# A decoder layer on one core: the cross layer's main loop begun four steps earlier, and the whole-row norms' bias formed by ScalarE

## The reference

```python
x = x + attn(_layernorm(x), Wqkv_w, Wqkv_b)         # 16 heads of 32, rotary, causal
x = x + xattn(_layernorm(x), ctx_2048, ...)         # a second norm _ln inside
x = x + ffn(_layernorm(x), w_gate_up, w_proj)       # ternary weights, silu, rms norm

def _L0_xattn_ref(...):
    ln_out = _ln(hidden_states, ln_w, ln_b)
    q  = _ln(_fp8_linear(ln_out, wq, q_in_scale))   # 8 groups x 2 heads x 128; k and v the same
    core = _gqa(q, k, v)                            # self half ("S")
    qx = _ln(_fp8_linear(ln_out, wqx, qx_in_scale))
    kx, vx = split(cond @ w_kv_x.T); kx = _ln(kx)
    xout = _gqa(qx, kx, vx)                         # context half ("X")
    catq = _div_clamp_fp8(cat([core, xout]), proj_smooth)
    return catq @ wproj.T * (proj_in_scale * proj_w_scale)
```

## Time and profile before

| | |
|---|---|
| median of 3 runs | 1286.97 us |
| lowest, highest | 1284.61, 3284.15 us |
| the profiled execution | 1285.17 us, its span 1283.4 |
| mean granted TensorE clock | 0.971 |
| PE busy | 1206.2 us, 94% |
| DVE busy | 943.5 us, 74% |
| ACT busy | 796.1 us, 62% |
| POOL busy | 624.7 us, 49% |

### The profile page before, as it was taken

One profiled execution on the slowest core, in us unless ns is written; L12 is line 12 of the kernel. 1 busy time (PEld: TensorE's weight loads), 2 busy tenths in 40 slices (PEclk: granted clock), 3 DMA queues, 4 the chain that ended last, 5 costly groups with the idle time before them and its releaser, 6 DMA issues.

```text
span 1283.4 us, 19499 instructions
## 1 busy us (share of the span) xinstructions
PE 1206.2 (94%) x6432; PEld 824.7 (64%) x6432; DVE 943.5 (74%) x2826; ACT 796.1 (62%) x2261; POOL 624.7 (49%) x786
## 2 busy tenths in 40 slices
PE   2999879789999999999999999999999998999998
PEld 1677657556676667676666776767677665555545
DVE  3769877799978886889999976557777877463341
ACT  3565535777777877666667765566787676652230
POOL 0838775653453455635556542125444534363470
PEclk9988877999999999999999999999999999899999
DMA  8311000001120222032332221041011110000000
GB/s 244 98 50 36 32 1 2 1 17 53 63 67 2 66 69 63 25 102 87 106 106 68 69 85 49 18 138 59 27 48 58 43 32 1 1 1 15 16 1 29
DMA packets 25460, 65.60 MB, mean 51 GB/s; under 512 B 2720, under 2 KB 8992, under 8 KB 25360
## 3 DMA queue, kind: packets, MB, share of 16 engines
q1 hardware_dynamic: 23776, 61.32, 15.4%
q10 hardware_dynamic: 1584, 3.05, 0.9%
HBM read 59.37 MB, written 4.98 MB: 50 GB/s over the span
## 4 chain that ended last, share of the span: by engine, by line
PE 61%; DVE 18%; ACT 12%; POOL 5%; issue 2%; DMA 2%; ACTq 0%; POOLq 0%; SPq 0%
PE ps L862 14%; PE ps L1059 8%; PE ps L1126 7%; PE ps L852 6%; PE ps L1021 5%; PE ps L954 4%; PE ps L1175 4%; ACT big L792 3%; PE ps L493 3%; PE ps L986 3%; DVE big L974 2%; PE ps L803 2%; DVE big L410 2%; PE ps L561 2%; ACT big L949 1%
## 5 line engine op out<-in xcount | busy, mean ns | idle before, releaser
L862 PE MATMUL ps<-big 128*125 128x512 bf16 x1152 | 264.5, 379 | 0.5 <-ACT big L949 0.5
L422 POOL TENSOR_TENSOR big<-big 112x4 f32<-112x4 f32 (+2 forms) x160 | 50.0, 312 | 422.1 <-ACT big L421 422.0
L792 ACT ACTIVATE big<-ps,big 112x128 f32<-112x128 f32 (+1 forms) x512 | 192.4, 456 | 71.6 <-POOL big L423 69.1
L862 PEld LDWEIGHTS ps<-big 128*125 128x125 bf16 x1152 | 155.2, 136 | 80.3 <-ACT big L949 0.8
L852 PE MATMUL ps<-big 128*112 128x512 bf16 x768 | 185.8, 385 | 1.8 <-POOL big L335 0.9
L852 PEld LDWEIGHTS ps<-big 128*112 128x112 bf16 x768 | 99.8, 132 | 65.3 <-issue 6.4
L974 DVE TENSOR_SCALAR big<-big 112x112 f32<-112x112 f32 (+1 forms) x256 | 130.2, 529 | 6.8
L651 POOL TENSOR_TENSOR big<-big 128x448 f32<-128x448 bf16 x96 | 102.2, 1065 | 67.3 <-DVE big L971 52.1
L410 DVE BATCH_NORM_STATS2 big<-ps 112x6 f32<-112x128 f32 (+1 forms) x512 | 113.1, 282 | 20.1 <-PE ps L862 18.7
L957 ACT ACTIVATE big<-ps,big 112x375 f32<-112x375 f32 x128 | 74.6, 583 | 82.6 <-DVE big L956 81.4
L1021 PE MATMUL ps<-big 125*128 125x224 f32 (+1 forms) x512 | 121.1, 359 | 2.5 <-DVE big L1003 1.7
(11 more groups left out here) (115 smaller groups left out, 2341.6 us busy)
## 6 DMA issues: line engine op xcount, KB each, us to landing
big<-in_ctx_t SPq DMA_DIRECT2D x32, 375.0 KB, 3.4
big<-in_w_s SPq DMA_DIRECT2D x16, 512.0 KB, 3.6
big<-in_w_p SPq DMA_DIRECT2D x16, 512.0 KB, 3.6
big<-in_w_x SPq DMA_DIRECT2D x16, 512.0 KB, 3.8
big<-in_w_g SPq DMA_DIRECT2D x16, 512.0 KB, 3.9
big<-in_w_d SPq DMA_DIRECT2D x8, 512.0 KB, 4.5
big<-in_w_a SPq DMA_DIRECT2D x8, 384.0 KB, 4.4
scr<-big SPq DMA_DIRECT2D x24, 128.0 KB, 1.7
```

What stands on the lines that cost most here:

```text
L792: t = act(lambda e, j=j: e.activation(z[0:rows, 128 * j:128 * j + 128], bk[0:rows, 128 * j:128 * j + 128], ACT.Identity, bias=rr[0:rows, 4 ...
L862: t = pe(lambda e, k=k, s=s, u=u, n=n: e.matmul(bk[0:CK, :], cT[:, s, k, CK * c:CK * c + CK], w[:, u, k, col:col + 512], start=n == 0, sto ...
```

## The change

1. `ln_rstd` for whole-row norms (n = 1) no longer uses POOL: ACT forms mean x r (Copy with a tile as scale) and its negative (Copy with scale -1). The norms per head stay as they were.
2. In `plan`, `l_0`, `l_1`, their `ln_r`, `l_0h` and `l_1h` stand one step earlier (lags lead+7 and lead+8 in place of lead+8 and lead+9). `l_2` and `l_q` stay.
3. The main loop begins after 34 steps of `run_a` in place of 38. `run_a` still has 53 steps, so 19 of them (34 to 52) now run beside the main loop, in place of 15.
4. Buffers move so that both fit: the first layer's weights to the upper half of `PW[0]`, its work area to the lower, `zl`, `az`, `fl` and the v slots elsewhere. The second half's weights wait, for the first 16 units, for what had been recorded at tick 14 (`a_mid`), the last 8 for the end of `run_a`.

```diff
+            if s["one"]:
+                t = act(lambda e: e.activation(s["q"], s["mean"], ACT.Copy, scale=r), t)
+                s["tr"] = [act(lambda e: e.activation(s["q"], s["q"], ACT.Copy, scale=-1.0), t)]
+                return s["i"], s["rr"], s["tr"]
             tq = pool(lambda e: e.tensor_tensor(s["q"], s["mean"], r, ALU.mult), t)
             s["tr"] = [t, pool(lambda e: e.tensor_scalar(s["q"], s["q"], -1.0, None, ALU.mult), tq)]
...
-        zl = Ring([f32(PW[0] + 512 * i, 512) for i in range(2)])
-        az = Ring([f32(PW[0] + 2048, 512)])
-        fl = Ring([f32(PW[0] + 1024 + 512 * i, 512) for i in range(2)])
-        aw = Area(PW[0] + 6144, 6144)
+        aw = Area(PW[0], 6144)
+        aH1 = aw.take(512)
+        zl = Ring([f32(a, 512) for a in (aH1, PW[0] + 8192)])
+        az = Ring([f32(PW[0] + 8192 + 512, 512)])
+        fl = Ring([f32(PW[0] + 8192 + 1024 + 512 * i, 512) for i in range(2)])
...
-        wA = w_view(PW[0], 4, 1536)
+        wA = w_view(PW[0] + 6144, 4, 1536)
...
-                (lead + 8, l_0),
+                (lead + 7, l_0),
+                (lead + 7, ln_r),
+                (lead + 8, l_1),
                 (lead + 8, ln_r),
-                (lead + 9, l_1),
-                (lead + 9, ln_r),
...
-                (lead + 9, l_1h),
-                (lead + 8, l_0h),
+                (lead + 8, l_1h),
+                (lead + 7, l_0h),
...
-        for n in range(4 * NB + A_LEAD + A_H - 8):
+        for n in range(T0):
...
-        bg = {LEAD + 7: prep_units("S1", PW[0], w_s[1], w_p[1], (0, 1, 2), lambda: a_end),
+        bg = {LEAD + 7: prep_units("S1", PW[0], w_s[1], w_p[1], (0, 1, 2), lambda: a_mid),
...
+        for u in bg[LEAD + 7][16:]:
+            u["free"] = lambda: a_end
```

More of the change, by code:

```diff
@@ L250, in prep_a @@
         def prep_a():
-            w = w_view(PW[0], 4, 1536)
+            w = w_view(PW[0] + 6144, 4, 1536)
             ready["a"] = []
@@ L414, in ln_stats @@
             return dict(i=i, rr=rr, r=rr[0:rows, 0:n], q=rr[0:rows, n:2 * n], mean=m2[:, :, 0], var=m2[:, :, 1],
-                        rows=rows, t=t2)
+                        rows=rows, one=n == 1, t=t2)
         def ln_rstd(s):
@@ L427, in decoder_layer @@
         marks = {}
-        zl = Ring([f32(PW[0] + 512 * i, 512) for i in range(2)])
-        az = Ring([f32(PW[0] + 2048, 512)])
-        fl = Ring([f32(PW[0] + 1024 + 512 * i, 512) for i in range(2)])
-        aw = Area(PW[0] + 6144, 6144)
+        aw = Area(PW[0], 6144)
[3 more added lines that the diff above has]
+        fl = Ring([f32(PW[0] + 8192 + 1024 + 512 * i, 512) for i in range(2)])
         ab = Area(aKV, 2432)
         ac = Area(a_att, sz_att)
-        wA = w_view(PW[0], 4, 1536)
+        wA = w_view(PW[0] + 6144, 4, 1536)
         a_bias = f32(ac.take(1536), 1536)
         t_bias = load(act_loads, a_bias[0:T, :], bias, s_bias, 16)
-        a_h1 = Ring([f32(aw.take(512), 512)])
+        a_h1 = Ring([f32(aH1, 512)])
         a_xT = Ring([b16(aw.take(448), 896).rearrange("p (s k t) -> p s k t", s=2, k=4) for _ in range(2)])
@@ L444, in decoder_layer @@
         a_p = Ring([f32(a.take(448), 448) for a in (aw, aw, ac, ac)])
+        ac.take(sz_att - 1536 - 4 * 448)
         a_pT = Ring([f32(a.take(448), 448).rearrange("p (j t) -> p j t", j=4) for a in (ac, ac)])
@@ L708, in l_q @@
                 it["fr"].release(fi, t1)
-        A_LEAD, A_H, A_Q = 10, 4, 14
+        A_LEAD, A_Q, T0 = 10, 14, 34
         def run_a():
@@ L762, in decoder_layer @@
         kS = Ring([f32(aKV + 448 * i, 448).rearrange("p (g t) -> p g t", g=4) for i in range(2)])
-        vS = Ring([f32(aKV + 896 + 512 * i, 512).rearrange("p (c n) -> p c n", c=1) for i in range(3)])
+        vS = Ring([f32(aKV + a, 512).rearrange("p (c n) -> p c n", c=1) for a in (1920, 896, 1408)])
         X_K1, X_V1 = aKV, aKV + 1500
@@ L1217, in all_now @@
             return [Tok(q.sem, q.count) for q in (pe, dve, act, pool)]
-        a_all, a_end = all_now(), []
+        a_all, a_mid, a_end = all_now(), [], []
         def free_rings(which, toks):
@@ L1261, in decoder_layer @@
             if next(tick_a, "end") == "end" and not a_end:
-                assert tick <= LEAD + 7
                 a_end.extend(all_now())
+            if tick == LEAD + 6:
+                a_mid.extend(all_now())
+            assert tick < LEAD + 23 or a_end
             if tick == LEAD:
```

## The result

| | before | changed |
|---|---|---|
| median | 1287.22 us | 1269.92 us |
| lowest | 1284.61 us | 1268.99 us |
| the profiled execution | 1285.17 us, span 1283.4 | 1269.07 us, span 1267.3 |
| mean granted clock | 0.971 | 0.977 |

The changed kernel takes 0.9878 of the time before (95% interval 0.9861 to 0.9896), 15.7 us less by that ratio, 16.1 in the profiled executions. 1267 had been forecast, with 1256 to 1280 as the range. The total came out right, but by luck: the experiments show that two terms of the sum were off by about 10 and 12 us, in opposite directions. What was booked to the earlier start belongs to the norms.

What follows compares the result with a forecast made beforehand. It took steps 34 to 52 as slack, no engine near full, with PE waiting for ACT's second norm behind POOL's queue. Gains 4 + 13 + 0.8 = 17.8 us off 1285.17 gave 1267, range 1256 to 1280.

Steps and rivals of the forecast that it cites:

- Which wait, and POOL's queue behind it: Cross layer: PE's gaps before transpose L687 end with ACT's second norm; 3.4 of the longest, 5.79 us, is POOL's queue.
- The norms one step earlier: Steps 21 to 33: waits on the second norm go, 4 us gained, between 0 and 6.3.
- The main loop at step 34: Steps 34 to 52: work that took 108.97 us takes 96, gain 13 us, bounds 0.4 and 17.4.
- Steps 42 to 52 at 53 us: Second part of the new stretch: 49.5 us of DVE work at 93% busy takes 53 us.
- Steps 34 to 41 at 43: First part of the new stretch: 43 us, between 40 (DVE 96%) and 49 (PE as slow as before); old time 46.85.
- the kernel is the old one four steps on: After step 52: nothing behind moves, the old kernel simply continues four steps on.
- Rival (a): Attention pulled in by the early start: POOL stretches DVE by 5 to 10 us, time 1273 to 1278; chance 0.13.
- Rival (b): Steps 34 to 52 bound by their chain, DVE staying at 80 to 83%, time 1277 to 1281; chance 0.10.
- (c): Better than forecast: PE keeps full clock, DVE's stretched instructions meet less POOL, time 1254 to 1261; chance 0.17.
- (d): Steps 42 to 52: attention delays ACT's first-layer work, 2.5 us a step, slower at 1294; chance 0.05.
- (e): Second norm late for DVE's sake, waits stay, steps 21 to 33 give 0, 1271 to 1273; inside forecast's 0.55.
- The last layer, 0.8 us: Last layer: PE's waits for ACT's norm L1078 shorten in 4 norms by 0.2 each, 0.8 us, bounds -0.4 and 1.6.

Runs made afterwards that it cites:

- e1: Kernel before with only the whole-row norms' bias formed by ScalarE instead of POOL; 1273.93 us, ratio 0.9921.
- e2: Kernel before with only the cross layer's whole-row norms one step earlier, bias still on POOL; 1274.27 us, ratio 0.9926.
- e4: Changed kernel with the main loop begun at step 38 again, so both norm edits without the earlier start; 1270.06 us, ratio 0.9889 to the kernel before.
- e3: Changed kernel without the two norm edits, so only the earlier main-loop start and its buffers; 1280.58 us, ratio 0.9964 to the kernel before.
- e7: Changed kernel without the clamp to 448 in the first-layer-side quantising, 32 VectorE instructions less; 1263.38 us, ratio 0.9827 to the kernel before.
- e7b: e7 with the main loop begun at step 38; 1264.56 us, ratio 0.9834 to the kernel before.
- e9: Changed kernel with the per-head norms' bias of the first half's first five batches on VectorE, not POOL; 1280.96 us, ratio 0.9965 to the kernel before.
- e10: As e9 on the changed kernel, but the VectorE instruction recorded two stages later, just ahead of the norm; 1275.25 us, ratio 0.9930 to the kernel before.
- e8: Changed kernel with one of two POOL instructions left out of 32 quantisings, DVE's list unchanged; 1258.53 us, ratio 0.9786 to the kernel before.
- e12: Changed kernel with the edits of e10 and e11 together; 1274.00 us, ratio 0.9920 to the kernel before.
- e13: e12 with the main loop begun at step 38; 1277.78 us, ratio 0.9945 to the kernel before.
- e11: Changed kernel with five copies of transposed exponentials (head group 1, batches 3 to 7) moved from VectorE to ScalarE; 1268.51 us, ratio 0.9874 to the kernel before.

## Why the prediction came out as it did

- **Which wait, and POOL's queue behind it**: right. The gaps ahead of L687 are gone, ACT no longer waits for POOL there, and e1 and e2 show that either edit removes most of it (10.2 and 9.5 us, both together 14.3).
- **"The norms one step earlier", 4 us with 6.3 as the bound**: this is the term that failed. I counted only the gaps inside steps 21 to 33 and bounded the gain by DVE's share of that stretch. By DVE's mark that stretch did give 4.2. But the waits of batches 4 to 7, 5.79 and 4.19 us among them, lie in steps 34 to 52, and I let their removal into the 96 us that I then booked to the earlier start. The norms with the bias measured 14.3 us (e4) where my sum had 4.8, 9.5 more.
- **"The main loop at step 34", 13 us**: mis-sized by about as much the other way, 11.6. It is 4.6 us alone (e3; 2.1 to 7.3 by its interval) and 1.4 beside the norms, which by the intervals can also be nothing. That the two errors cancel to 2.1 us, 15.7 measured for 17.8, is luck: the forecast of the total rests on a split that is wrong. My sum set the new stretch against 108.97 us, old stretch and four steps, as if the norms left that time alone. The balance of e4 shows they had already brought DVE from 35.0 us idle to 18.0, and the start left 17.9. Why 18 us remain whichever step it begins at stays open; e7 and e7b, with 22.1 and 21.4, rule out that it is only a matter of DVE's load.
- **Steps 42 to 52 at 53 us**: 53.5, though not at 93% of 49.5 us of DVE work but at 96% of 51.3. **Steps 34 to 41 at 43**: 47.3. The new gap of 4.43 at 186.74 is as large as the 4.3 us missing; that it is the same time is not shown, since e9 and e10, which took POOL out of this wait and shortened it to 1.7 and 2.3 us, lost more elsewhere. The prediction named a stall behind POOL's queue only for whole-row norms; L426 and L427 stayed on the same queue for the per-head ones, which the early start brings beside the first layer's rotary. The question "what is late next" had the answer in the diff: the function has two callers, and only one was changed.
- **After step 52 "the kernel is the old one four steps on"**: off by 3.0 us at step 56 and by 2.0 at the thirty-third projection (62.51 against 60.48). A mark on PE takes no account of DVE's backlog; part of what PE gains ahead of it is given back.
- **Rival (a), DVE stretched by POOL**: not as priced. It was to come from the attention brought in by the early start, with 5 to 10 us, and to show as over 92 us of DVE in steps 34 to 52; it was 90.15. DVE does need 3.05 us more in the balance (216.03 against 212.98), but not for the start: with the norm edits alone it is 216.79 (e4), with the second of them alone 215.66 (e2), with the start alone 213.55 (e3). The attention's L974 takes 422 ns on the mean before and 421 after. That POOL's work lengthens DVE's instructions is shown by e8. The Trainium skill, "GPSIMD Engine Reference" (its table of specifications), names this contention without a size; here L654 goes from 0.54 to 0.44 us when one of two POOL instructions is left out of 32 quantisings.
- **Rival (b)**, DVE at 80 to 83%: no, 89% over steps 34 to 52, at 5.3 us a step, where I had said 5.0 and, for (b), 5.6. Still, DVE stands idle for 18 us, 11.8 of them waiting for PE (5.8 for the scores L567, 3.3 for L590, 2.7 for L992), and no run shows what would shorten these waits. **(c)**: no; the clock between 122 and 222 us rose from 0.81 only to 0.88, where I had said above 0.9, and DVE's busy time for the same instructions rose instead of falling. **(d)**, slower: no. **(e)**, that the waits stay: no.
- **The last layer, 0.8 us**: ACT's idle time before the norm (L1078, now L1084) fell from 5.6 us to 0.4, but PE's waits for it are 7.9 us against 8.1. From the first transposes of this layer to its first output group it is 83.5 us against 84.1. The term has about the right size: this stretch takes 84.1 to 84.3 us in the three profiles with the bias on POOL (before, e2, e3) and 82.1 to 83.6 in the eleven with it on ACT. What it rests on, PE's waits, hardly moved, so how the saving arises stays open.
- **Not forecast**: 1.7 us of the profiled difference at the very end, shown below, which goes with no edit.

## What to carry to other kernels

When two edits of a change act on the same stretch, set up the sum once with each edit alone; a wait that the first one removes must not be counted again in what the second saves. Take the balance on the engine that holds the other end of the stretch (here DVE, 92% full in the changed kernel; PE's busy time moves with its clock), as length less busy time over one piece of work with fixed ends: it said at once what each edit did (35.0 us idle before, 23.7 in e1, 20.7 in e2, 32.6 in e3, 18.0 in e4, 17.9 in the changed kernel), where marks on the engine that runs ahead misled by 2 to 3 us. Compare the profiled execution with its kernel's median first, as e3, e12 and e13 show. And before an instruction is moved onto that engine, ask what it waits for: 15 instructions of 0.23 us that each waited 1 us for another engine made this kernel 11 us slower.

## What the runs showed of the hardware

The stretching of DVE beside POOL follows POOL's work, not DVE's: with 32 DVE instructions left out (e7) the two neighbours grew by 0.11 and 0.12 us each and half of the saving was lost; with 32 POOL instructions left out (e8) 609 unchanged DVE instructions took 10.9 us less.

The clock fell at the end in some executions and not in others, with the same instructions: the granted clock was 0.96 from 1244 us to the end in the profile of the kernel before and 1.00 from 1230 us on in that of the changed one. Of PE's last output groups, 32 matmuls each, the first behind the gap and the next, in the kernel before, and then in the changed kernel:

```profile
1249.04 8.77 PE L1175 MATMUL ps<-big 128*112 128x512 bf16 x32 [2.30 <-DVE big L1147]
...
1257.78 7.09 PE L1175 MATMUL ps<-big 128*112 128x512 bf16 x32
```

```profile
1234.64 7.08 PE L1181 MATMUL ps<-big 128*112 128x512 bf16 x32 [2.30 <-DVE big L1153]
...
1241.69 7.09 PE L1181 MATMUL ps<-big 128*112 128x512 bf16 x32
```

8.77 us against 7.08, after the same gap of 2.30 us. Of the experiments' profiles, e1, e2, e3, e7b, e9, e12 and e13 show the long first group, e4, e7, e8, e10 and e11 do not, so it does not go with any edit. 1.7 us of the difference between two profiled executions of this kernel can be this alone.
